# A decoder layer with eight experts on one core: each expert's 641 rows as five tiles of 128 and one odd row, the last scaling on VectorE

## What is computed

```python
logits = xf @ wg                                    # xf: 4096 tokens of 128 features
scores = softmax(logits); top1 = argmax(scores)     # one expert per token
rank = position of the token among those of its expert
valid = rank < capacity                             # capacity = int(4096 / 8 * 1.25) + 1 = 641
buf[top1 * capacity + rank] = xf
h = gelu(einsum('ecd,edf->ecf', eb, W1) + b1)       # eb: 8 x 641 x 128, W1: 8 x 128 x 512
y = einsum('ecf,efd->ecd', h, W2) + b2              # W2: 8 x 512 x 128
out = where(valid, y[slot], 0) * combine_w
x = layernorm(x + out)
```

## Time and profile before

| what | value |
|---|---|
| median of 3 runs | 499.87 us (498.59 to 501.1) |
| the profiled execution: its own time, its span | 499.5 us, 497.6 us |
| busy in the span: PE, DVE, ACT, POOL | 425.5, 358.0, 283.5, 247.6 us |
| first part: last scatter into `expert_in` issued | at 381.2 us |
| `EB` of the first expert landed, PE goes on | at 389.3 us |
| second layer of the first expert begins | at 398.6 us |
| one expert, from first layer to next first layer | 10.44 us |
| last matmul | ends at 477.2 us |
| last indirect DMA issued by POOL | ends at 490.7 us |

### The profile page before, as it was taken

How to read it: one execution, slowest core, us unless ns; L and a number is a source line. 1 busy time by engine, 2 the same in 40 slices (tenths; PEclk the granted TensorE clock), 3 DMA queues, 4 the chain that set the end, 5 groups by cost and what they waited for, 6 DMA issues and landing times. The chain is left out here.

```text
span 497.6 us, 20822 instructions
## 1 busy us (share of the span) xinstructions
PE 425.5 (86%) x7767; PEld 335.0 (67%) x7767; DVE 358.0 (72%) x1680; ACT 283.5 (57%) x691; POOL 247.6 (50%) x420
## 2 busy tenths in 40 slices
PE   3879999999999999999999999998851699999930
PEld 2667777777777777777777777775641488888730
DVE  5255677788888788888788888887574267767740
ACT  1445667666766666767666766666242356666620
POOL 4132244554454554454554454553364036887883
PEclk9999999999999999999999999999775699999985
DMA  5700000101000101000101000000004333344100
GB/s 149 237 14 14 24 14 14 29 25 38 27 24 26 29 25 40 25 26 24 30 24 40 26 13 15 19 15 19 13 29 121 84 81 89 101 112 124 24 19 18
DMA packets 30901, 22.69 MB, mean 46 GB/s; under 512 B 4460, under 2 KB 27281, under 8 KB 30804
## 3 DMA queue, kind: packets, MB, share of 16 engines
q1 hardware_dynamic: 27604, 17.16, 12.3%
q0 software_dynamic: 3200, 4.22, 2.9%
HBM read 12.25 MB, written 9.65 MB: 44 GB/s over the span
## 5 line engine op out<-in xcount | busy, mean ns | idle before, releaser
L1007 DVE TENSOR_REDUCE mx<-banks 128x8 f32<-128x1024 f32 x64 | 75.4, 1219 | 37.8 <-PE banks L541 37.8
L797 ACT ACTIVATE arena<-banks 128x1024 f32<-128x1024 f32 x64 | 62.0, 1021 | 35.4 <-PE banks L541 35.4
L426 POOL TENSOR_TENSOR rs<-ve,minus_half 128x1 f32<-128x1 f32 x32 | 18.0, 564 | 115.5 <-DVE ve L977 115.5
L589 PE MATMUL banks<-arena,V 128*32 128x128 f32 x2048 | 70.0, 278 | 0.6 <-ACT arena L797 0.6
L767 ACT ACTIVATE arena<-banks,first_half 128x512 f32<-128x512 f32 x64 | 44.7, 698 | 32.8 <-PE banks L541 32.8
L589 PEld LDWEIGHTS banks<-arena,V 128*32 128x32 f32 x2048 | 52.6, 110 | 11.1 <-issue 8.9
L483 POOL DMA_INDIRECT out_x<-ot,idx x48 | 50.0, 1041 | 12.0 <-issue 10.2
L533 PE MATMUL banks<-CE,x1T 32*128 32x128 f32 x1024 | 37.5, 282 | 10.7 <-DVE x1T L1088 9.7
L437 POOL TENSOR_TENSOR rs<-ve,minus_half 128x1 f32<-128x1 f32 x32 | 17.9, 559 | 56.1 <-DVE ve L996 56.0
L745 PE MATMUL banks<-w_sb,arena 128*112 128x128 f32 (+1 forms) x384 | 44.0, 274 | 0.9 <-issue 0.6
L533 PEld LDWEIGHTS banks<-CE,x1T 32*128 32x128 f32 x1024 | 32.2, 186 | 18.2 <-DVE x1T L1088 16.2
(11 more groups left out here) (149 smaller groups left out, 1039.2 us busy)
## 6 DMA issues: line engine op xcount, KB each, us to landing
w_sb<-in_L_ffn_W SPq DMA_DIRECT2D x16, 256.0 KB
expert_in<-zeros SPq DMA_DIRECT2D x10, 273.0 KB, 3.3
EB<-expert_in SPq DMA_DIRECT2D x8, 341.2 KB
X<-in_x SPq DMA_DIRECT2D x32, 64.0 KB, 1.9
C<-in_ctx SPq DMA_DIRECT2D x32, 64.0 KB, 2.3
out_x<-fb SPq DMA_DIRECT2D x32, 64.0 KB
out_x<-ot,idx POOLq DMA_INDIRECT x48
b2b<-in_L_ffn_b SPq DMA_DIRECT2D x1, 512.0 KB, 5.2
```

The source lines that it names most:

```text
L589: mm = pe.matmul(bank(name)[VW * s:VW * (s + 1), half * P:(half + 1) * P], V[:, h, :], scored[:, h // NA, h % NA, :], start=q == 0, stop=q ...
L797: nc.scalar.activation(P2[b % 2][:, 2 * half:2 * half + 2].rearrange("p j a t -> p j (a t)"), pair("s2t", half), ACT.Exp, scale=SCALE).the ...
L1007: v.tensor_reduce(mx[b % 2][:, 8 * half:8 * half + 8].rearrange("p (j a) -> p j a", a=NA), pair("s2", half).rearrange("p j (a t) -> p j a ...
```

## The change

The second part is tiled anew. An expert's first 640 rows are `ET` = 5 tiles of 128, with row 5p + c in partition p of tile c, so that each partition of `EB` is one contiguous piece of 5 x 130 numbers. The 641st row of all eight experts is loaded by one more DMA into `ER` (8 x 130) and transposed once. In the first layer it is column 640 (halves of 321 and 320 columns). In the second layer its four chunks are four matmuls of 32 weight columns in four column groups of the array, first in each expert's sequence (L787), and DVE copies the result to `parts`. At the last expert eight matmuls against `odd_part` (zeros and ones, L771) sum the four groups and pick the rows. The scaling moves from ACT to DVE as a `tensor_scalar` of two operations on SBUF (L1241), `shifted` is dropped, groups are of two and three tiles, POOL's order is written anew, and 16 matmuls of the identity run on PE (L743) before it waits for the first `EB`.

```diff
-    ER = 112
-    ET = -(-CAP // ER)
-    CAPP = ER * ET
+    ET = CAP // P
+    JT = ET + 1
+    ROWS = ET * P + 1
+    HALVES = [(0, 321), (321, ROWS)]
+    CAPP = 656
+    WARM = 16
...
+        GROUPS = [(e, tiles) for e in range(E) for tiles in ([0, 1], [2, 3, 4])]
...
-                sp.dma_start(EB[e % 3][:], buf[e * CAPP:(e + 1) * CAPP, :].rearrange("(c p) d -> p c d", p=ER)).then_inc(
+                sp.dma_start(EB[e % 3][:], buf[e * CAPP:e * CAPP + ET * P, :].rearrange("(p c) d -> p c d", c=ET)).then_inc(
                     eb_in[e % 3], 16)
...
-            for e in range(3):
+            expert_rows(0)
+            sp.dma_start(ER[:], buf.rearrange("(e c) d -> e c d", c=CAPP)[:, ET * P, :]).then_inc(er_in, 16)
+            for e in range(1, 3):
                 expert_rows(e)
...
-            for n in range(GROUPS):
-                root(n)
-                if n >= LATE:
-                    scatter(n - LATE)
-            for n in range(GROUPS - LATE, GROUPS):
-                scatter(n)
+            for e in range(E):
+                root(2 * e)
+                scatter(2 * e, [0])
+                root(2 * e + 1)
+                if e == E - 1:
+                    root_rest()
+                scatter(2 * e, [1])
+                scatter(2 * e + 1, [0, 1, 2])
+            scatter_rest()
...
+            for _ in range(WARM):
+                pe.matmul(act_bank[0][:, 0:P], ident[:], ident[:], start=True, stop=True)
...
             def second_layer(e):
+
+                if e == E - 1:
+                    pe.wait_ge(t_done, 2 * E)
+                    pe.wait_ge(y_done, (E - 2) * JT + 1)
+                    for k in range(E - 1):
+                        odd_rows(k, False)
                 pe.wait_ge(h_done, 2 * FC * (e + 1))
...
+                        if k == 0:
+                            mm = pe.matmul(max_bank[i % 2][VW * f:VW * (f + 1), 0:D], hT[e % 2][:, f, ROWS - VW:ROWS],
+                                           w2_sb[e % 2][:, f, :], start=True, stop=True, tile_position=(0, VW * f))
...
-                for n in range(max(0, (e - 1) * PER + 1), e * PER + 1):
-                    scaled(n)
-            for n in range((E - 1) * PER + 1, E * PER):
-                scaled(n)
...
+            def scaled(n):
+                e, tiles = GROUPS[n]
                 dve.wait_ge(rstd3_ready, n + 1)
...
+                for t, c in enumerate(tiles):
+                    v.tensor_scalar(ot[n % 4][:, t, :], r3[e % 2][:, c, :], mv3[e % 2][:, c, 0:1], rs3[e % 2][:, c:c + 1],
+                                    ALU.subtract, ALU.mult).then_inc(ot_ready, 1)
...
+            for e in range(E):
+                if e > 0:
+                    spread_of(e - 1, ET - 1, stats(e - 1, ET - 1))
+                gate_mark = gated(e)
+                token_rows(e)
+                if e == 0:
+                    rest_mark = rest_gated()
                 else:
-                    summed(i, gate_mark)
-                    spread_of(i - 1, mark)
...
+                    scaled(2 * e - 1)
+                if e + 1 < E:
+                    rows_turned(e + 1)
+                parts_copied(e)
+                for c in range(ET):
+                    if c > 0:
+                        mark = stats(e, c - 1)
+                    summed(e, c, gate_mark)
+                    if c > 0:
+                        spread_of(e, c - 1, mark)
+                if e < E - 1:
+                    scaled(2 * e)
+            spread_of(E - 1, ET - 1, stats(E - 1, ET - 1))
+            scaled(2 * E - 2)
+            rest_summed(rest_mark)
+            scaled(2 * E - 1)
```

More of the change, by code:

```diff
@@ L204, in decoder, with late @@
         w2_sb = ring("w2_sb", 2, [P, FC, D])
-        EB = ring("EB", 3, [ER, ET, DR])
-        def late(at, rows, d0, d1):
-            end = at + 2 * d0 * d1
-            assert end <= 4 * SC
-            return [arena[0:rows, at + k * d0 * d1:at + (k + 1) * d0 * d1].rearrange("p (a b) -> p a b", a=d0)
-                    for k in range(2)], end
-        ebT, end = late(0, P, ET, ER)
-        hT, end = late(end, P, FC, USED)
-        xg, end = late(end, ER, ET, D)
+        EB = ring("EB", 3, [P, ET, DR])
+        ER = sb("odd_rows", [E, DR])
+        b2r = sb("b2r", [E, D])
+        def late(at, shape):
+            size = math.prod(shape)
+            assert at + 2 * size <= 4 * SC
+            parts = [arena[:, at + k * size:at + (k + 1) * size] for k in range(2)]
+            if len(shape) == 2:
+                parts = [part.rearrange("p (a b) -> p a b", a=shape[0]) for part in parts]
+            return parts, at + 2 * size
+        ebT, end = late(0, [ROWS])
+        hT, end = late(end, [FC, ROWS])
+        xg, end = late(end, [ET, D])
         act_bank = [banks[:, k, :] for k in range(4)]
@@ L367, in _ @@
             for k in range(4):
-                sp.wait_ge(out_done[k], 16 * GT * (GROUPS // 4))
+                sp.wait_ge(out_done[k], 16 * sum(len(GROUPS[n][1]) for n in range(k, len(GROUPS), 4)))
+            sp.wait_ge(rest_out, 16)
         @block.gpsimd
@@ L728, in first_layer @@
                 pe.wait_ge(w_in[e % 2], 32 * (e // 2 + 1))
-                rows = ebT[e % 2][:].rearrange("p c r -> p (c r)")
                 for f in range(FC):
-                    for half in range(2):
+                    for half, (r0, r1) in enumerate(HALVES):
                         j = 2 * FC * e + 2 * f + half
@@ L900, in _ @@
             own.wait()
+            own.mark(v.memset(odd_part[:], 0.0))
+            own.wait()
+            v.tensor_copy(odd_part[:].rearrange("p a b -> p (a b)")[:, 0:E * E:E + 1], lane[:, VW - 1:VW].broadcast_to([P, E]))
             v.tensor_scalar(minus_head[:], lane_pair[:].unsqueeze(2).broadcast_to([P, NA, P]), -1.0, None, ALU.mult)
@@ L1190, in spread_of @@
-            def spread_of(i, mark):
-                e, c = i // ET, i % ET
-                rows = tile_rows(c)
-                own.wait(mark)
-                own.mark(v.bn_aggr(mv3[e % 2][0:rows, c, :], st3[0:rows, i % GT, :]))
-                if i % GT == GT - 1:
-                    own.wait()
-                    v.tensor_scalar(ve3[e % 2][:, c + 1 - GT:c + 1], mv3[e % 2][:, c + 1 - GT:c + 1, 1], LN_EPS, None,
-                                    ALU.add).then_inc(var3_ready, 1)
-            for tile in mv3:
-                own.mark(v.memset(tile[:], 0.0))
@@ L1229, in _, with stats, spread_of @@
-            spread_of(E * ET - 1, stats(E * ET - 1))
-            shifted(GROUPS - 1)
+            def stats(e, c):
+                dve.wait_ge(y_done, e * JT + 2 + c)
+                return own.mark(v.bn_stats(st3[:, c % 2, :], r3[e % 2][:, c, :]))
+            def spread_of(e, c, mark):
+                own.wait(mark)
+                own.mark(v.bn_aggr(mv3[e % 2][:, c, :], st3[:, c % 2, :]))
+                for of, tiles in GROUPS:
+                    if of == e and tiles[-1] == c:
+                        own.wait()
+                        group = slice(tiles[0], c + 1)
+                        v.tensor_scalar(ve3[e % 2][:, group], mv3[e % 2][:, group, 1], LN_EPS, None,
+                                        ALU.add).then_inc(var3_ready, 1)
```

213 lines of the change are left out of this document (110 added, 103 removed).

## The result

| | before | after |
|---|---|---|
| median (9 runs each) | 499.69 us | 505.38 us |
| profiled execution: its time, its span | 499.5, 497.6 us | 505.1, 503.4 us |
| PE's transposes of the first expert begin | 389.3 us | 391.1 us |
| first layer of the first expert begins | 391.4 us | 393.5 us |
| one expert, from the second on | 10.44 us | 11.27 to 11.34 us |

The ratio is 1.0115, with an interval of 1.009 to 1.0141: slower by 1.2%, where I had forecast 1.4% faster. One of the nine runs of the changed kernel took 784.55 us, far from the others' 502.64 to 508.22, and is not in the ratio. The ratio holds for this first measurement.

A forecast was written before the change was run, and what follows sets the result against it. PE, waiting only for ACT's gelus, was taken as the bound: 5.11 us of first layer and gelus plus 5.33 of second layer per expert. PE -3.3, POOL -2.9, clock -0.5 gave -6.7 and 493.0 us, range 490.0 to 497.0.

The forecast's parts named there:

- PE's saving: Second part: PE's gain in the second layers less the cost of the odd rows, -3.3 us together.
- Second layer: Each expert's second layer: column groups replace the sixth tile, 5.33 to 4.79 us; 4.3 us less for eight experts.
- rival 4: Second layer: the column groups don't overlap, or each is a pass of its own; 498.1 us, chance 0.07.
- Odd rows: Behind the last first layer: seven extra matmuls cost 0.77 us, the eighth 0.22; together +1.0 us.
- POOL: After PE's last issue: POOL's last DMA ends 10.8 us later instead of 13.7; -2.9 us.
- DVE: Second part: VectorE's added scalings and copies fit, with one wait for POOL within 0.8 us in hand; cost 0.
- rivals 2 and 3: Second part: DVE late and PE stalls; mildly, 494.5 to 496.5 us (chance 0.14), or fully, 503 us (0.07).
- Clock: Front: the clock probably falls again before the first layer; -0.5 us for the part done at the high level.
- Rival 1: Front: the clock stays high until the first expert; 491.0 us, chance 0.17.
- First part: The part before 380 us: the change leaves it alone, so nothing was counted for it.

The follow-up runs named there:

- changed_again: The changed kernel unedited, run once more on another chip as a control: 492.61 us, ratio 0.9867 to the kernel before.
- no_warm: The changed kernel without the 16 identity matmuls ahead of the wait for `EB`: 505.08 us.
- own_signals_warm24: own_signals with 24 identity matmuls instead of 16 ahead of the wait for `EB`: 503.52 us, ratio 1.005 to the kernel before.
- two_per_signal: The changed kernel with two semaphores per group of output DMAs instead of one: 506.68 us, ratio 1.0142 to the kernel before.
- before_again: The kernel before, unedited, profiled once more on the third chip: one execution with a span of 504.2 us.
- spread: The changed kernel with POOL's indirect DMAs spread over an expert, at most three between two roots: 494.11 us; on another chip 495.87 us.
- own_signals: The changed kernel with a semaphore of its own for each tile of a group's output DMAs: 494.45 us, ratio 0.9916 to the kernel before.
- old_order: The changed kernel with POOL's order of the kernel before (a root, then the whole group two back): 501.04 us, ratio 1.0025 to the kernel before.
- full_pass: The changed kernel with each expert's odd row in passes of the whole array, without column groups: 505.56 us, ratio 1.0078 to the kernel before.

## Why the prediction was wrong, and where it was right

On a chip without late tiles the kernel does what I forecast: 492.6 us against 493.0, and a span of 491.1 - 497.6 = -6.5 against -6.7. That it comes this close is in part luck: PE's saving fell short by 1.4 us and the clock's 0.5 did not come, while an earlier start of the first layer gave 1.4 and POOL 0.2 more. Changed_again beside the earlier trace rows:

- *Second layer, -4.3.* From the second expert on 10.03 us instead of the 9.90 forecast: the groups take 0.36 (forecast 0.35), the five tiles 4.57 (forecast 4.44). The first expert gave 0.34. So 7 x 0.41 + 0.34 = 3.2 less, short by 1.1. The groups overlap, and rival 4 is out.
- *Odd rows, +1.0.* The last expert took 462.30 to 473.60, 1.27 more than the others: +1.3 instead of +1.0.
- *POOL, -2.9.* From PE's last issue to POOL's last DMA 473.60 to 484.83 = 11.2 (forecast 10.8), so 2.5 less; and from there to the end of the span 6.3 instead of 6.9, another 0.6 less. The odd-row DMA took 0.89 us, just below the range of 0.9 to 1.4. In the first measurement it is 497.08 - 485.84 = 11.2 as well:

```profile
494.91 0.97 POOL L497 DMA_INDIRECT out_x<-ot,idx  x1 [0.30 <-issue]
496.19 0.89 POOL L508 DMA_INDIRECT out_x<-otr,idxr  x1 [0.30 <-issue]
```

- *DVE, 0.* Right: the three scalings waited 0.51 for POOL's root and took 0.86 together, and `parts` was copied at 438.03, before PE needed it. The three ran from 436.12 to 436.98, over the first 0.7 us of POOL's DMA at 436.29, and weren't held up. So rivals 2 and 3 did not come. The prediction's reading that the second half of any indirect DMA holds VectorE up went too far: in the kernel before each of the six long ones of L1152 (0.58 to 0.60 us, the other at a DMA 0.16) met a DMA of 82 rows (1.41 to 1.42 us), and the changed kernel has none of those. By the rule of the Trainium skill (SBUF — State Buffer, "Who interferes with whom") the second and third scaling, if they run in a 2-port mode, should have waited for the DMA instruction; the trace disagrees here.
- *Clock, -0.5.* Wrong for both profiles of the changed kernel, where it is 0. The clock rose on the matmuls and had fallen again by the first expert's first layer, which took 6.81 us (below) and 6.66 in changed_again. It took 6.59 in the kernel before, 6.09 in no_warm and 7.50 with 24 matmuls (own_signals_warm24), but single profiles differ too much for a ranking: fifteen of the sixteen with 16 matmuls lie between 6.00 and 7.60.

```profile
382.63 6.28 PE L743 MATMUL banks<-ident 128*128 128x128 f32 x32 [1.13 <-DVE x L1117]
391.10 1.29 PE L752 MATMUL banks<-ident,EB 128*128 128x128 f32 x5 [2.19 <-DMA EB<-expert_in]
393.49 6.81 PE L766 MATMUL banks<-arena,w_sb 128*128 128x321 f32 x16 [0.89 <-DVE arena L1183]
```

- *Rival 1* did come in the sixteenth, two_per_signal: its granted clock is 1.00 from 386 us on through the first layer (last row: PE, PEld, DVE, ACT, POOL busy, PEclk, DMA share, GB/s).

```profile
388.96 0.77 PE L755 MATMUL banks<-ident,EB 128*128 128x128 f32 x5 [2.31 <-DMA EB<-expert_in]
390.93 4.59 PE L769 MATMUL banks<-arena,w_sb 128*128 128x321 f32 x16 [1.05 <-DVE arena L1186]
390.90:395.30 4.40, 4.37 (x16) 3.09 (x17) 1.99 (x10) 3.46 (x7) 0.00 (x0) 1.00 0.01 4
```

  From the transposes to the second first layer that is 12.10 us instead of the 14.62 of changed_again, the 2.5 that the prediction gave for a clock held throughout. Why it held in this one is open: the idle time before the transposes, 2.31 us, is like that of the others (1.38 to 3.73).
- *First part, 0.* Here it isn't. The kernel before has one long step, number 16 (11.36 us). Every changed kernel has two, numbers 12 and 14 (11.32 to 11.36 each on the chips with late tiles, 10.99 to 11.01 on the others), and step 16 is short; why they move wasn't looked for. That is 0.8 us more where tiles are late and 0.1 in changed_again. Beside it the start varies from one execution to the next: the first expert's first layer began between 388.8 and 397.4 us, and in changed_again 1.4 us earlier than in the profile before, which is the other half of the cancelling. before_again is the latest of them. 4.9 of its 6.1 us are in steps 3 and 4 (12.63 and 11.82 us instead of 9.65 and 9.90), at a granted clock of 0.50 from 30 to 40 us, and 1.6 in a longer wait for `EB`; against that, its step 16 is 0.4 shorter. Its PEclk, in tenths, shows that low stretch, which the earlier trace rows doesn't have:

```profile
PEclk9958999999999999999999999999675599999985
```

**The step that failed** in the first measurement is "*Second layer*: ... an expert 5.11 + 4.79 = 9.90". It took for granted that VectorE sees a tile 0.2 us after PE's last pass. The runs showed in its place 0.8 us of waiting ahead of three sums per expert, 11.3 us an expert. Beside changed_again, whose span is 12.3 us shorter, that is 6 x 1.27 = 7.6 in the experts but the first and last, 0.9 in the last one, and 3.6 in when the first layer began (393.49 against 389.92). Of these 3.6, 0.7 are steps 12 and 14, late signals again; the rest I count as chance. I had written down idle time of PE at L790 with DVE as releaser as the sign of rivals 2 and 3. The sign came, but it named the wrong engine: behind VectorE stood PE again. None of my rivals had a signal between two idle engines arrive late, and POOL's term let it in: I priced its new order by the length of its work alone, though the change had also put four DMAs in a row where PE has only two banks to work with.

What could have been seen beforehand is little. In the kernel before VectorE waited for PE in the second layers too, so the hand-over was already on the way, but only 9 times and for 2.0 us in all (from 404 to 466 us), 0.44 at most:

```profile
DVE r L1179 <- PE banks L745: 2.0, 9, 0.4
```

A late signal that its trace does have, ScalarE's wait of 1.07 us in step 16 of the first part, can be told only beside another chip's, 0.71 us at the same place in before_again.

## What to carry to other kernels

When engine A waits for B and B for A in the same rows, look for the signal between them, and give the ring one buffer more to see it bare. Don't credit an edit with a gain before the unedited kernel has run on the same chip: spread and own_signals had clean runs behind them, and so had the unedited kernel on such a chip. (POOL's order does matter on a chip with late tiles: 10.24 to 10.28 us per expert in old_order against 11.27 to 11.35 in full_pass on the same chip.) And look for a part of the trace that no edit touches: here one step of the first part tells which kind of chip it is. A tight hand-over (two banks, 0.2 us) makes a kernel's time depend on such things; the kernel before, whose DMAs come two in a row, had medians within 0.3% of each other on all seven later chips.

## What was not expected of the hardware

- On some chips a finished matmul tile reaches the engine that waits for it late while POOL issues indirect DMAs: ScalarE by 0.36 us with a single one in the first part, VectorE by up to 2.3 us in runs of three and four (1.28 us apart) and by over 5 us in a run of eight. It happens with hardly any data moved, and no tile is late with plain DMAs. On other chips the same program shows nothing of it: 505.4 us against 492.6.
- 16 matmuls that PE ran ahead of a wait raised its clock each time, but in one of sixteen profiles only was it still high for the first layer (4.59 us; 6.00 to 7.60 in the others).
